# A decoder layer's three stages in one kernel: all engines' orders and the banks laid out anew, products of a zero tile in the first pairs' waits

## What is computed

```python
x = _layernorm(x + attn(x, Wq, bq, Wk, bk, Wv, bv, Wo, bo, q_gain))
x = _layernorm(x + wkv(time_decay, time_first, k=x, v=ctx_2048))
x = _layernorm(x + ffn(x, up_weight, down_weight, up_scale, down_scale, output_scale))

def attn(x):   # 16 query heads, 4 key/value heads, 16 channels each
    q, k, v = heads(x @ Wq.T + bq), heads(x @ Wk.T + bk), heads(x @ Wv.T + bv)
    q, k = rope(rms_norm(q)) * q_gain, rope(rms_norm(k))
    a = softmax(causal(q @ k.T * HD ** -0.5))
    return (a @ v) @ Wo.T + bo

def ffn(x):    # 256 -> 1024 -> 256
    hidden = relu((x @ sign(up_weight).T) * up_scale)
    return (hidden @ sign(down_weight).T) * down_scale * output_scale
```

## Time and profile before

| | us |
|---|---|
| median of 3 runs | 209.41 (207.58 to 209.79) |
| profiled execution | 209.36 |
| its span, first to last instruction | 207.5 |
| busy: TensorE, VectorE, ScalarE, GpSimd | 164.4, 168.7, 149.3, 125.6 |

### The profile page before, as it was taken

The page is one execution under the profiler, slowest core; times in us unless marked ns, Lnnn a source line. Parts: engine busy times, 40 slices in busy tenths (PEclk is TensorE's granted clock), DMA queues, the critical chain, the costliest instruction groups (busy, mean ns, idle before and its releaser), DMA issues. The chain is left out here.

```text
span 207.5 us, 4218 instructions
## 1 busy us (share of the span) xinstructions
PE 164.4 (79%) x1375; PEld 108.4 (52%) x1375; DVE 168.7 (81%) x343; ACT 149.3 (72%) x280; POOL 125.6 (61%) x185
## 2 busy tenths in 40 slices
PE   6965238999578989899979979697998967598940
PEld 2432112635326737674756556396756765476820
DVE  2747783558988999989999999899989999897560
ACT  0363373799965798967798869768987888486932
POOL 8489405024566464094696528987987979764622
PEclk9999757999958999999999999999999999999996
DMA  6285905023008004400610081008410010010111
GB/s 215 60 300 183 292 17 123 0 51 80 0 8 223 2 0 82 148 0 5 128 50 3 0 190 41 0 2 190 145 47 7 0 51 3 0 51 11 46 54 54
DMA packets 19198, 14.84 MB, mean 72 GB/s; under 512 B 14307, under 2 KB 14563, under 8 KB 18918
## 3 DMA queue, kind: packets, MB, share of 16 engines
q1 hardware_dynamic: 18448, 14.43, 24.7%
q10 hardware_dynamic: 726, 0.11, 0.3%
HBM read 9.29 MB, written 2.10 MB: 55 GB/s over the span
## 5 line engine op out<-in xcount | busy, mean ns | idle before, releaser
L886 ACT ACTIVATE probs<-banks 128x1024 f32<-128x1024 f32 x32 | 31.6, 1025 | 2.6 <-PE banks L370 2.5
L462 PE MATMUL banks<-x2hi,up_sb 128*128 128x256 f16 x128 | 29.5, 273 | 3.4 <-DVE x2lo L1641 3.2
L475 PE MATMUL banks<-dn_sb,hid_hi 128*128 128x256 bf16 x128 | 29.6, 274 | 2.3 <-DVE r L1572 1.2
L954 ACT ACTIVATE hid<-banks,ups_man 128x256 f32<-128x256 f32 x64 | 26.4, 470 | 5.9 <-PE banks L462 5.5
L475 PE MATMUL banks<-dn_sb,hid_lo 128*128 128x256 bf16 x128 | 29.5, 273 | 0.0
L462 PE MATMUL banks<-x2lo,up_sb 128*128 128x256 f16 x128 | 29.5, 273 | 0.0
L323 PE MATMUL banks<-wqkv_sb,xT_sb 128*128 128x384 f32 x64 | 24.7, 533 | 3.0 <-ACT qk L846 2.0
L1277 POOL TENSOR_TENSOR hid_lo<-hid,hid_hi 128x512 f16<-128x512 f32 x16 | 20.7, 1296 | 4.5 <-ACT hid_hi L961 4.4
L1190 POOL TENSOR_SCALAR veps<-mv 128x2 f32<-128x2 f32 x24 | 10.7, 445 | 20.8 <-DVE mv L1587 19.8
L392 PE MATMUL banks<-probs,v_sb 128*32 128x512 f32 x128 | 19.2, 704 | 5.0 <-ACT probs L886 5.0
L1199 POOL TENSOR_TENSOR rstd<-veps,half_neg 128x2 f32<-128x2 f32 x24 | 21.7, 906 | 0.6
(11 more groups left out here) (124 smaller groups left out, 408.0 us busy)
## 6 DMA issues: line engine op xcount, KB each, us to landing
xT_sb<-xT_dram SPq DMA_DIRECT2D x8, 256.0 KB, 3.2
x_sb<-x_dram SPq DMA_DIRECT2D x8, 256.0 KB, 3.4
ctxT_sb<-ctxT_dram SPq DMA_DIRECT2D x8, 256.0 KB, 3.6
out_dram<-outb SPq DMA_DIRECT2D x8, 256.0 KB, 2.1
up_f<-up_dram SPq DMA_DIRECT2D x1, 1024.0 KB, 5.0
dn_f<-down_dram SPq DMA_DIRECT2D x1, 1024.0 KB, 7.0
wqkv_sb<-wqkv_dram SPq DMA_DIRECT2D x1, 384.0 KB, 3.7
wo_sb<-wo_dram SPq DMA_DIRECT2D x1, 256.0 KB, 3.8
```

The costliest lines, as they stand in the source:

```text
L462: mm = nc.tensor.matmul(banks[:, UP[n], s * T * S:(s + 1) * T * S], up_sb[:, c, j * 128:(j + 1) * 128], part[:, c, :, :].rearrange("p t s ...
L475: mm = nc.tensor.matmul(banks[:, DN, t * D:(t + 1) * D], part[:, j, t * S:(t + 1) * S], dn_sb[:, j, :], start=(j == 0 and t == 0 and m == ...
L886: nc.scalar.activation(probs[:, KVH * (m // 2) + m % 2:KVH * (m // 2) + m % 2 + 3:2].rearrange("p n j s -> p n (j s)"), banks[:, SC[m]:SC[ ...
L954: nc.scalar.activation(hid[:, j, :], banks[:, UP[n], (j % 2) * T * S:(j % 2 + 1) * T * S], ACT.Relu, scale=ups_man[:, j:j + 1]).then_inc(s ...
```

## The change

Four things are changed.

1. Banks: SC is (2, 6, 2, 6), so that `exps(p, 0)` and `exps(p, 2)` read banks 2 and 3, and `exps(p, 1)` and `exps(p, 3)` banks 6 and 7. `products(p, 0)` (bank 3) and `products(p, 1)` (bank 2) then wait for the third exponential of the pair to free the bank; products(p, 1) still waits for the fourth for its data.
2. The Newton step of pair 0 goes from GpSimd to VectorE. At the start VectorE also takes the sines of pair 0 and the cosines and rope sum of pair 1, and GpSimd the cosines of pair 0.
3. TensorE runs products of the zero tile: six behind project(1), eight behind project(2), eight between scores(0, 0) and scores(0, 1), three behind those, and four, into bank 3, right before products(2, 0) and behind its wait. The flag's load and the branch stand before project(2) instead of behind it.
4. The lists of all engines are written in another order from pair 0 to pair 7. What each function does is unchanged.

TensorE at the start, before: from project(2) (L323) to the first products (L392).

The diff, cut to its core:

```diff
-        SC = (6, 2, 6, 2)
-        NEWTON_ON_DVE = (1, )
+        SC = (2, 6, 2, 6)
+        NEWTON_ON_DVE = (0, 1, )
...
@@ SyncE @@
+            store(0)
             head_rows(6)
             next_x(5)
             next_ctx(5)
-            store(0)
...
@@ TensorE @@
-            def keep_busy(n):
+            def keep_busy(n, bank):
 
                 pe.wait_ge(idle_ready, 1)
                 for k in range(n):
-                    nc.tensor.matmul(banks[:, X1], idle_b[:, 0:128], idle_b[:], start=True, stop=True)
+                    nc.tensor.matmul(banks[:, bank], idle_b[:, 0:128], idle_b[:], start=True, stop=True)
...
-            keep_busy(7)
+            keep_busy(7, X1)
             project(0)
             pe.wait_ge(sems["qk_out"], 1)
             pe.wait_ge(sems["v_out"], 1)
             project(1)
-            pe.wait_ge(sems["qk_out"], 2)
-            pe.wait_ge(sems["v_out"], 2)
-            project(2)
+            keep_busy(6, X1)
             pe.wait_ge(setup_dve, GUARD_SET)
             plain_flag.append(pe.value_load(plain[0:1, 0:1], min_val=0, max_val=1))
 
             def remaining(guarded):
 
+                pe.wait_ge(sems["qk_out"], 2)
+                pe.wait_ge(sems["v_out"], 2)
+                project(2)
                 pe.wait_ge(masks_ready, MASKS)
+                keep_busy(8, X1)
                 if guarded:
                     row_scores(0)
                 scores(0, 0, guarded)
+                keep_busy(8, X1)
                 pe.wait_ge(sems["probs_done"], 2)
                 scores(0, 1, guarded)
-                pe.wait_ge(sems["probs_done"], 4)
+                keep_busy(3, X1)
+                pe.wait_ge(sems["probs_done"], 3)
                 products(0, 0)
-                pe.wait_ge(sems["probs_done"], 4)
+                pe.wait_ge(sems["probs_done"], 3)
                 products(0, 1)
...
                 scores(2, 1, guarded)
-                pe.wait_ge(sems["probs_done"], 12)
+                pe.wait_ge(sems["probs_done"], 11)
+                keep_busy(4, PV[0])
                 products(2, 0)
...
                 ffn_up(7, 0)
-                ffn_down(6, 3)
                 pe.wait_ge(sems["hid_done"], 56)
                 ffn_up(7, 1)
+                ffn_down(6, 3)
...
@@ ScalarE; first_guess(2) ahead of both take_products of pair 0 @@
             exps(0, 3)
+            first_guess(2)
             take_products(0, 0)
-            first_guess(2)
             take_products(0, 1)
-            mixer_constants()
+            take_values(2)
             take_channels(0)
...
@@ ScalarE, pair 2 and the signs @@
-            take_values(3)
-            squares(3)
+            first_guess(3)
             signs()
-            first_guess(3)
             take_channels(1)
+            take_heads(4)
             exps(2, 0)
-            take_heads(4)
+            log_den(0)
             exps(2, 1)
-            log_den(0)
-            squares(4)
             first_rec(0)
+            high_heads(3)
             exps(2, 2)
             exps(2, 3)
-            high_heads(3)
...
             exps(3, 1)
-            relu(0, 0)
-            log_den(1)
-            relu(0, 1)
-            first_rec(1)
+            high_heads(4)
             exps(3, 2)
             exps(3, 3)
...
@@ GpSimd @@
             attention_constants()
-            rope_sines(0)
-            newton_rms(0)
+            rope_cosines(0)
             scan_pads()
-            rope_cosines(1)
             guard_constants()
-            rope_sum(1)
             rope_sum(2)
             newton_rms(2)
...
-            add_out(6)
+            low_bits(7, 0)
             low_bits(7, 1)
...
@@ VectorE @@
             gains_constants()
+            rope_sines(0)
             head_sums(0)
-            rope_cosines(0)
+            newton_rms(0)
             rope_sum(0)
             scale_heads(0)
...
-            small_constants()
+            rope_cosines(1)
             head_sums(1)
+            rope_sum(1)
             newton_rms(1)
-            head_sums(2)
             scale_heads(1)
...
             attend_norm(0, 1)
             with dve.If(guard_flag[0]):
                 row_maxima(1)
+            small_constants()
             scale_heads(2)
-            mixer_constants()
             residual(0)
...
             scale_out(6)
-            low_bits(7, 0)
+            add_out(6)
```

458 lines of the change are left out of this document (228 added, 230 removed).

## The result

The changed kernel takes 202.36 us (median of 5 runs, 201.34 to 205.59), the kernel before 209.41 us. The ratio is 0.9666, 95% interval 0.963 to 0.9703: faster, by 7.05 us. The forecast was 203.7 us with a range of 199.8 to 207.9. The profiled execution took 201.34 us (span 199.60), so the two profiled spans differ by 7.9 us; it is the fastest of the five and 1.0 us under their median, and what set it apart comes with e7.

The account below looks back on a forecast made before the run. VectorE, 95% busy, was taken to bound the middle; the start was one chain through pair 0's attention. Terms -5.4 - 0.5 + 0.5 - 0.25 = -5.65 took 209.36 to 203.7 us, range 199.8 to 207.9.

Parts of the forecast that it names:

- Term 1: The start, through pair 0's attention: scan(0) at 44.2 instead of 49.65 us, -5.4 us, bounds -2.4 to -6.2.
- the stack is ready 0.65 us earlier: Start, VectorE: with pair 0's Newton step there, qn starts at 15.3 against 15.95; scores(0, 0) at 21.95.
- `small_constants` stands here, 3.5 us as before: Start, VectorE: moved behind attend_norm(0, 1), it is covered by pair 0's output projection, save 0.8 us of scale_heads(2).
- All covered at full clock: Start, TensorE: zero products around pair 0's scores fit its waits; at 1.2 GHz the second eight would hold scores(0, 1) 1.7 us.
- rival C: Zero products don't hold TensorE's clock, in pair 0's scores and products and at pair 2: +5.0 us, 208.7; chance 0.06.
- Term 2: Second clock loss, at products(2, *): shorter TensorE wait, clock should hold; -0.5 us, bounds -1.4 and +1.8.
- Term 3: The middle, scan(0) to the tail: same VectorE instructions reordered, possible new waits; +0.5 us, bounds -6.6 and +8.
- Term 4: The tail: ffn_up(7, 1) no longer behind ffn_down(6, 3), ScalarE's 0.24 us before its second relus goes; -0.25 us.
- A: The middle eats the lead: VectorE waits for ScalarE in the new order; four us of new waits, 207.7; chance 0.10.
- B: Slower: low_bits on VectorE wait for high_bits behind ScalarE's exponentials; six pairs, 10.2 us, 213.9; chance 0.07.
- D: TensorE's branch lasts as long as the weights load, delaying project(2): 204.4 or 206 us; counted within the forecast's 0.67.
- E: The order also removes most of the middle's idle time: 4 us more, 199.7; chance 0.10.

Follow-up runs that it names:

- e7: Changed kernel with small_constants back in its old place on VectorE, between swap_keys(0) and pair 1's cosines; 202.31 us, ratio 0.9684.
- e1: New order up to scan(0), old order of everything behind it, with the new banks; 208.49 us, ratio 0.9975 to the kernel before.
- e4: Changed kernel with the old score banks, SC = (6, 2, 6, 2), and the waits that go with them; 213.09 us, ratio 1.0206.
- e5: e1 with more zero products of TensorE, ahead of products(2, 0) and in two waits for pair 6; 205.24 us, ratio 0.9824.
- e6: e4 with the fourth exponential moved right behind the third on ScalarE in pairs 1, 5, 6 and 7; 209.20 us, ratio 0.9995.
- e3: Changed kernel without the added zero products, keeping only the seven at the very start; 204.60 us, ratio 0.9809.
- e2: Old kernel up to scan(0), with the new order of everything behind it and the new banks; 208.97 us, ratio 1.0031.
- e11: e10 with project(0)'s bias added from the f32 row and the gain constants moved behind head_sums(0); 202.19 us, ratio 0.967.
- e9: Kernel before with zero products added ahead of pair 0's scores and products and ahead of products(2, 0); 208.39 us, ratio 0.9935.
- e10: Changed kernel with pair 0's cosines moved to VectorE and more zero products at the start and in the tail's waits; 201.08 us, ratio 0.9625.

## Why the prediction was right, and where it was not

The forecast was 1.3 us over the measured time, and the sign and the size of the largest part were right. By its own steps:

- **Term 1, -5.4; measured -4.79.** The step that failed is "the stack is ready 0.65 us earlier". It counted the sines at nothing beside GpSimd's cosines; they took 2.28 us for 0.89, held up the head sum, and y came at 13.97, not at 13.55. In this execution project(1) also took 4.51 us, since the clock fell at 11 us, and ScalarE's heads, values and squares of pair 1 stand ahead of high_heads(0). The last copy into the stack started at 18.54, in before at 18.43, and in e1, e4, e5, e6 and e7, with the sines as slow or nearly so and project(1) at full pace, at 18.24 to 18.30: the step was worth 0.13 to 0.19 us, not 0.65. The rows landed at 22.69, not 21.95. From there the steps came close to what was said: scores to exponentials 0.89 us (forecast 0.8), exps(0, 0) to exps(0, 2) 2.89 (2.75), on to the products 1.08 (1.0), on to r 7.88 (8.5), on to scan(0) 9.43 (9.2). But the scores to exponentials kept this pace only because the clock held: in e1, e5 and e7 it did not, the steps from the scores to exps(0, 2) took 4.9 to 5.1 us for 3.8, and the term was -3.7 to -3.9.
- **The second step that failed: "`small_constants` stands here, 3.5 us as before".** It took 1.15 us, and e7 shows that its place is worth nothing that can be measured. The forecast read a stretched duration as the operations' own price, and put down to the order what was GpSimd's work beside them. As the step cost the sum at most the 0.8 us by which it held up scale_heads(2), the error hardly shows in Term 1; as a reason it was wrong.
- **The zero products hold the clock: right in the profiled execution, not in each.** "All covered at full clock" left out what TensorE waits behind the eight ahead of scores(0, 0): 2.66 to 2.69 us in e1, e5 and e7, where the clock fell and the next eight took 2.69 to 2.90 us for 1.90. So a part of rival C (its price 5.0 us) happened there, at 0.9 to 1.05 us. The 3.3 us that the rows gave for clock losses agree with what the zero products are worth (e3: 3.0 us) in the sum and not by parts: 2.7 us at the start (1.9 from the rows) and 0.74 us at pair 2 (1.4). In the old order the loss at pair 2 cost nothing that shows (17.32 us with it, 17.38 us in e5 without). The rule of the Trainium skill, TensorE: Matmul & The Clock Gate, section Part 1: The HAM clock gate, which the prediction weighed against them (a ramp under 1% of a span, under 2.1 us here), came out low: e3 gives 3.0 us, and e5 against e1 3.1 us.
- **Term 2, -0.5; measured -0.52** from scan(0) to scan(1), with TensorE's waits at 1.10 and 1.22 us (forecast near 1.5). By e3 the clock is worth 0.74 us of it and the new order costs 0.22 us (17.54 against 17.32).
- **Term 3, +0.5; measured -2.35.** This is the term that was mis-sized, with the wrong sign. "VectorE has the same instructions between scan(0) and the tail" is where it went wrong, together with the count of waits alone. From scan(0) to scan(7) VectorE's idle time did grow, from 6.56 to 7.18 us, but its busy time fell from 117.67 to 114.18 us. 1.09 us of that are two bn_stats and two bn_aggr that now stand behind scan(7), in the tail, where VectorE has 5.4 us of waits to put them in. Most of the rest are operations that, as I read it, GpSimd's work no longer stretches, less some that it now does (the scans, +1.06 us): the nine hid_lo 1.24 us less, the seven guess 1.29 us, the copies of the stack 0.55 us less. One such pair from before:

```profile
116.60 1.76 DVE L1685 TENSOR_TENSOR guess<-ratio,rec 128x512 f32<-128x512 f32 x1
```

```profile
116.53 1.28 POOL L1271 TENSOR_TENSOR newt<-ratio,rec 128x512 f32<-128x512 f32 x1 [3.06 <-ACT rec L925]
```

  In the changed kernel the same guess takes 0.69 us at 111.86, before GpSimd's newt (112.56). e2 and e3 show that the 104.6 us belong to the order with its banks, not to the start or the zero products. How the 2.35 us divide between work moved and work less stretched I read from the two traces; no run separated them. That GpSimd contends with a VectorE operation that has two inputs in SBUF is also what the Trainium skill, GPSIMD Engine Reference, section 1. Specifications, says.
- **"In the middle TensorE isn't the bound, so I count nothing" (of the banks): wrong as a reason.** e4 puts 5.6% on the exchange within this order, some of it through the clock.
- **Term 4, -0.25; measured -0.24**: ScalarE's gap ahead of the second pair of relus is gone.
- **Rivals.** A (the middle eats the lead) did not happen in the changed kernel, and did in e1, by a mechanism that it had not named: the clock. B did not happen (low_bits 0.2 us in all). D did not (project(2) at 16.48 us). E was right in its direction and not in its mechanism: the middle also gained, 2.9 of its 4 us, while VectorE's idle time grew.

The forecast was right in part by fortune. The changed kernel keeps its clock through TensorE's waits of 2.38 and 2.30 us in the tail, and e2, with the same code and waits, does not. By the table that is 1.6 us (34.93 against 33.38), and nothing in the profile of before said on which side it would fall. And errors offset each other: Term 1 came out 0.6 us short (1.5 to 1.7 us with the start of e1, e5 and e7) and Term 3 2.85 us the other way.

## What to carry to other kernels

Cut two profiles at the same recurring instruction and compare the stretches: here it showed that the middle keeps its length whatever start stands before it, and that clock losses of 1 to 2 us lie over it. Before half of a change is called worthless, look whether TensorE's clock was lost somewhere else, fill that wait and time it again. Filling behind the wait was enough here behind 1.22 and 1.74 us (e7, e5), though once it was not (e11), and too late behind 2.65 us (e9). Treat the duration of a small VectorE operation as its price only where GpSimd was idle beside it, and where an order is laid out for a bank or buffer plan, change both or neither.

## What the runs showed of the hardware that I had not expected

- The same two waits of TensorE (2.38 and 2.30 us, 1.5 us apart) cost the clock in e2 and not in the changed kernel; in e1 waits of 2.33 and 1.25 us cost it, in before 2.33 and 1.43 us did not. What decides is not the length alone.
- One kernel divides by this: e10's executions were 200.75 to 201.15 us, or 202.2 and 202.29; the profiled one of the latter had lost the clock at 61 to 64 us. The mean granted clock of the whole execution is 0.984 in both of the longer ones and 0.988 to 0.990 in the four others.
- Twelve zero products in the tail's two waits took 1.7 us off e1's tail, though they do no work; four behind a wait of 2.65 us did not save the products after them (3.22 us).
- The granted clock in the records is 1.00 in the first microseconds, yet the seven zero products there stand 0.45 us apart, twice the 0.24 us of later ones:

```profile
1.30 3.12 PE L314 MATMUL banks<-idle_b 128*128 128x512 bf16 x7 [1.30 <-POOL idle_b L1182]
```

- Ordinary f32 operations of VectorE beside GpSimd's took far longer: two sines 2.28 for 0.89 us, a guess 1.76 for 0.69 us, the small k_bias 1.47 for 0.17 us. GpSimd's operation beside them kept its length (1.54, 1.28 and 1.53 us). It can be the other way round: in the changed kernel a guess that started at 52.02 took 0.69 us, and GpSimd's newt, started at 52.06, took 1.77 us for 1.27. In these cases one of the two pays, not both.
